# Keeping the products of |gate| and its sigmoid in the up stage of an attention and quantized-FFN kernel, gate signs parked apart, no sweeps on GpSimd

## The chip, the cores and the metric

One core of a Trainium2 chip. A core has TensorE (matmul), VectorE (DVE), ScalarE (ACT), GpSimd (POOL) and SyncE (SP, here the only engine that issues DMAs). The metric is the device time of one execution in microseconds.

## What is computed

x is 2 x 2048 x 512 in f32. A layer norm, cross attention against a context of 128 rows, a residual; then a layer norm, a gated feed-forward net whose weights are quantized in blocks of 32 and whose activations are rounded with one scale for the whole tensor, and a residual:

```
def act_qdq(x):
    qmax = 2.0 ** (ACT_BITS - 1) - 1.0
    scale = jnp.maximum(jnp.max(jnp.abs(x)) / qmax, 1e-12)
    return jnp.clip(jnp.round(x / scale), -qmax - 1.0, qmax) * scale
...
x = act_qdq(x)
up = act_qdq(x @ lpbq_dequant(w_up).T)
gate = act_qdq(x @ lpbq_dequant(w_gate).T)
sig = fixed_qdq_u16(jax.nn.sigmoid(gate))
gate = act_qdq(gate * sig)
o = act_qdq(gate * up)
return o @ lpbq_dequant(w_down).T
```

Each act_qdq needs the maximum of the absolute value over the whole tensor before one element can be rounded. gate, up, gate * sig and o are 4096 x 1536; each of them therefore needs a pass that finds a maximum and a later pass that uses it.

## The kernel before

A tensor of 4096 x 1536 is handled as NU = 48 tiles of 128 partitions x 1024 elements (512 KB in f32). Eight groups of 512 tokens (NG) have six tiles each (UPG). One tile of a product is one unit: 24 matmuls (two halves, four chunks of the contraction, three pairs of high and low f16 parts, L623).

The stages, in order of time:

- *Attention and norms* (to about 137 us), with the weights' quantization beside them.
- *Gate product* (gate, take_gate, gate_max, park_gate). TensorE computes unit after unit into two pairs of PSUM banks; ScalarE copies each out (L682), VectorE takes its maximum (L1100), SyncE stores it in gate_park in DRAM. Two groups also turn the up and down weights. At its end come the maximum over the partitions, an all-reduce on GpSimd (L404), and the scale ginv (quant_scale, L1070).
- *Up product*, in two passes over the gate beside it. Pass a, with up units 0 to 23, two gate tiles each: SyncE fetches a gate tile; GpSimd rounds it to int16 into Q (gate_int, L464); ScalarE takes the magnitude (sweep_a, L811) and the sigmoid (sigmoid, L816); VectorE rounds the sigmoid (L1137) and multiplies and takes the maximum in one instruction (act_max, L1149; the product is written and not used). Then the scale sinv. Pass b, with units 24 to 47: the sigmoid again (L825), its rounding, and the rounded gate * sig into Q, on VectorE for even tiles (L1156) and on GpSimd (L475, L478) and VectorE (L1162) for odd ones. Beside both, ScalarE copies each up unit out of PSUM (take_up), VectorE takes its maximum (up_max, L1132) and SyncE stores it in up_park (L290). Unit n may start in PSUM when unit n-2 is out. At the end: the scale uinv.
- *The maximum of o* (676 to 777 us), in which TensorE has nothing to do. SyncE reads the 48 up tiles back (L327) into a ring of six; ScalarE takes |up| (L865) and |Q| (L851) for three tiles of four and VectorE multiplies with the maximum (L1217); the fourth goes over GpSimd (L488) and VectorE (L1208, L1210). Then the scale oinv, and the down weights and first up tiles are loaded.
- *Down product*: SyncE reads each up tile again, ScalarE rounds it (up_int, L883), VectorE multiplies with Q (o_int, L1238), splits the result in two f16 parts (L1241, L1243), TensorE multiplies (L665), VectorE adds the residual (finish, L1249), SyncE stores.

SyncE's queue is one list in program order: a DMA behind a wait is not issued before that wait is over. The same holds on every engine. Q keeps gate * sig for all 48 tiles as int16 with its sign, in 24,576 words per partition; the up tiles don't fit beside it, so they are read back from DRAM twice.

## Time and profile before

| | us |
|---|---|
| three runs: median (lowest to highest) | 1036.32 (1035.14 to 1036.73) |
| the profiled execution, its own time | 1034.82 |
| its span | 1033.0 |
| gate product, about | 137 to 398 |
| up product, about | 398 to 676 |
| maximum of o, about | 676 to 777 |
| down product, about | 777 to 1033 |

The span is from the first to the last instruction that the profiler saw. The stages' ends are read from the first and last matmul of each. Times in the rows below count from the span's start.

### The profile page before, as it was taken

The numbers are of one execution on the slowest core, as the hardware profiler recorded it, in microseconds if no ns is written. First come the engines' busy times: TensorE is split into PE (matmuls) and PEld (weight loads), VectorE is DVE, ScalarE is ACT, GpSimd is POOL, SyncE is SP. The second block draws the span as 40 slices with busy tenths as digits, with TensorE's granted clock in tenths as the row PEclk, the third lists the DMA queues.
The fourth block names the chain that finished last, engine by engine and source line by source line (L and its number), as shares of the span: only waits on it lengthen the run. The fifth ranks groups of instructions, "written<-read, shape, count | busy, mean of one in ns | idle before, by whom it ended". The sixth has DMA issues, their size and how long they took to land.

```text
span 1033.0 us, 12734 instructions
## 1 busy us (share of the span) xinstructions
PE 885.3 (86%) x4344; PEld 443.5 (43%) x4344; DVE 691.8 (67%) x957; ACT 497.7 (48%) x621; POOL 307.8 (30%) x218
## 2 busy tenths in 40 slices
PE   7999779999999999889996999910008999999998
PEld 6788534445444544333342444400003444444443
DVE  4999967423352332999997999969989744456610
ACT  2489854123221323889995656558984311222100
POOL 0399800660048001546563556512110000000000
PEclk9999999999999999999999899965558999999999
DMA  9522342222522274678891234228999744456221
GB/s 349 241 113 94 123 163 102 102 102 95 210 103 102 82 264 164 227 245 260 279 274 78 102 134 191 102 84 308 302 336 329 233 149 141 154 203 203 81 81 41
DMA packets 47706, 179.32 MB, mean 174 GB/s; under 512 B 4784, under 2 KB 4784, under 8 KB 45488
## 3 DMA queue, kind: packets, MB, share of 16 engines
q1 hardware_dynamic: 47664, 178.80, 48.6%
q8 instruction: 21, 0.34, 0.1%
q14 instruction: 21, 0.17, 0.0%
HBM read 108.53 MB, written 70.25 MB: 173 GB/s over the span
## 4 chain that ended last, share of the span: by engine, by line
PE 69%; issue 13%; DVE 9%; ACT 4%; DMA 3%; POOL 1%; POOLq 0%; SPq 0%; ACTq 0%; DVEq 0%
PE ps L623 35%; PE ps L665 24%; PE ps L495 4%; DVE big L1217 3%; PE ps L556 2%; ACT big L816 2%; PE ps L573 2%; DVE big L1149 2%; ACT big L682 1%; DVE big L1208 1%; DMA big<-up_park 1%; DMA big<-gate_park 1%; PE ps L513 1%; DVE small L1137 1%; DMA big<-in_L_xattn_Wq_dram 1%
## 5 line engine op out<-in xcount | busy, mean ns | idle before, releaser
L623 PE MATMUL ps<-big 128*128 (+1 forms) x2304 | 507.4, 381 | 27.5 <-ACT big L682 22.7
L623 PEld LDWEIGHTS ps<-big 128*128 128x128 f16 x2304 | 223.8, 98 | 306.2 <-ACT big L682 30.0
L665 PE MATMUL ps<-big 128*128 128x512 f16 x1152 | 251.2, 382 | 101.7 <-DVE big L1243 101.7
L682 ACT ACTIVATE big<-ps 128x1024 f32<-128x1024 f32 (+2 forms) x216 | 163.8, 787 | 286.4 <-PE ps L623 208.8
L665 PEld LDWEIGHTS ps<-big 128*128 128x128 f16 x1152 | 113.0, 98 | 239.8 <-issue 105.4
L1100 DVE TENSOR_REDUCE small<-big 128x1 f32<-128x1024 f32 (+1 forms) x48 | 58.4, 1219 | 147.7 <-ACT big L682 147.6
L883 ACT ACTIVATE big<-big,small 128x1024 int16<-128x1024 f32 x48 | 55.0, 1148 | 152.2 <-DVE big L1238 145.6
L1249 DVE SCALAR_TENSOR_TENSOR big<-ps,small,big 128x1024 f32<-128x1024 f32 x16 | 20.5, 1284 | 118.9 <-PE ps L665 118.9
L464 POOL TENSOR_SCALAR big<-big,small 128x1024 int16<-128x1024 f32 x48 | 78.7, 1641 | 66.1 <-DMA big<-gate_park 57.2
L495 PE MATMUL ps<-small,big 128*128 128x128 f32 x456 | 64.2, 283 | 11.0 <-DMA big<-in_ctx_dram 4.6
L404 POOL PARTITION_ALL_REDUCE small<-small x9 | 3.3, 380 | 225.2 <-DVE small L930 118.8
L495 PEld LDWEIGHTS ps<-small,big 128*128 128x128 f32 x456 | 54.4, 145 | 24.6 <-ACT big L682 8.0
L1238 DVE SCALAR_TENSOR_TENSOR big<-big,small 128x1024 int16<-128x1024 int16 x48 | 61.4, 1278 | 1.2 <-ACT big L883 1.1
L1132 DVE TENSOR_REDUCE small<-big 128x1 f32<-128x1024 f32 (+1 forms) x48 | 57.9, 1206 | 0.0
L816 ACT ACTIVATE big<-big,small 128x1024 f32<-128x1024 int16 x48 | 54.9, 1143 | 5.3 <-POOL big L464 2.9
L1217 DVE CUSTOM_DVE_ANT_0 big<-big,small 128x1024 f32<-128x1024 int16 x36 | 53.7, 1535 | 0.5 <-ACT big L851 0.4
L825 ACT ACTIVATE big<-big,small 128x1024 f32 (+1 forms) x48 | 52.2, 1139 | 0.0
L1137 DVE TENSOR_SCALAR small<-big 128x1024 uint16<-128x1024 f32 x54 | 42.7, 791 | 11.4 <-ACT big L816 10.1
L865 ACT ACTIVATE big<-big,small 128x1024 int16<-128x1024 f32 x36 | 41.0, 1143 | 18.8 <-DMA big<-up_park 8.5
L811 ACT ACTIVATE small<-big,small 128x1024 int16<-128x1024 f32 x36 | 41.1, 1143 | 9.7 <-DVE small L1149 9.4
L475 POOL TENSOR_SCALAR big<-big,small 128x1024 f32<-128x1024 int16 x24 | 35.2, 1468 | 34.7 <-DVE big L1162 27.7
L1149 DVE CUSTOM_DVE_ANT_0 big<-small 128x1024 f32<-128x1024 int16 x24 | 39.9, 1663 | 0.9
(90 smaller groups left out, 850.4 us busy)
## 6 DMA issues: line engine op xcount, KB each, us to landing
big<-up_park SPq DMA_DIRECT2D x96, 512.0 KB, 4.7
gate_park<-big SPq DMA_DIRECT2D x48, 512.0 KB, 2.6
big<-gate_park SPq DMA_DIRECT2D x48, 512.0 KB, 4.2
up_park<-big SPq DMA_DIRECT2D x48, 512.0 KB, 2.7
big<-in_x_dram SPq DMA_DIRECT2D x8, 1024.0 KB, 17.6
x_park<-big SPq DMA_DIRECT2D x8, 1024.0 KB, 3.9
big<-x_park SPq DMA_DIRECT2D x16, 512.0 KB, 4.5
out_dram<-big SPq DMA_DIRECT2D x16, 512.0 KB, 2.7
```

Of the source, the lines that this page charges most:

```text
L464: nc.gpsimd.tensor_scalar(Q[:, v], gate_in(v % 6, v >= 36), col["ginv"], 1.0, ALU.mult, ALU.mult).then_inc(q_d, 1)
L495: return nc.tensor.transpose(dst, src, ident)
L623: mm = nc.tensor.matmul(ps[:, 2 * (n % 2) + j], w[:, a, k, o:o + P], XT[:, g, b, k], start=(k == 0 and a + b == 0), stop=(k == KC - 1 and ...
L665: mm = nc.tensor.matmul(ps[:, 4 * s + i], OT[:, s, a, c, i * P:(i + 1) * P], WD[:, b, c], start=(c == 0 and a + b == 0), stop=(c == OC - 1 ...
L682: return nc.scalar.activation(dst, src, ACT.Copy)
L816: nc.scalar.activation(gate_in(v % 6, v >= 36), Q[:, v], ACT.Sigmoid, scale=col["gsc"]).then_inc(sig_d, 1)
L883: nc.scalar.activation(qa[:, k % 2], ring6[:, s], ACT.Copy, scale=col["uinv"]).then_inc(uq_d, 1)
L1100: nc.vector.tensor_reduce(gcol[:, bass.ds(g * UPG + n, 1)], gate_out[:, n % 2], AX.X, ALU.max, apply_absolute_value=True).then_inc(g_mx, 1)
L1132: nc.vector.tensor_reduce(ucol[:, bass.ds(n, 1)], up_out[:, s], AX.X, ALU.max, apply_absolute_value=True).then_inc(u_mx, 1)
L1149: nc.vector.tensor_tensor_reduce(gate_in(v % 6, v >= 36), magnitude(v), sig_int(v), 1.0, scol[:, s:s + 1], ALU.mult, ALU.max, scol[:, s:s ...
L1217: nc.vector.tensor_tensor_reduce(ring5[:, k % 6], qa5[:, k % 4], qb5[:, k % 4], 1.0, ocol[:, c:c + 1], ALU.mult, ALU.max, ocol[:, c:c + 1] ...
L1238: nc.vector.scalar_tensor_tensor(qb[:, k % 2], qa[:, k % 2], col["oinv"], Q[:, n], ALU.mult, ALU.mult).then_inc(oq_d, 1)
```

## The change

- Each gate tile is swept once. The rounded gate (now on ScalarE for every third tile, on VectorE for the others), its magnitude (ScalarE), the sigmoid (ScalarE), the rounded sigmoid and the product with its maximum (VectorE) are made as before, but the product |gate| * sigmoid, in f32, is kept. When its scale is known it is only scaled and rounded (settle), on ScalarE and VectorE in turn.
- 23 products stay in SBUF on a "shelf" (the words of Q), 25 go to a "bench" (the words of the up product's input, as its groups are used up); the 16 of these that come first are stored in product_park and fetched back.
- The sweep takes three gate tiles per two up units, over up units 0 to 31; the scaling takes six tiles per unit, in units 33 to 40.
- The product has lost the gate's sign. So in the gate product ScalarE also makes the sign of each tile as int16 (ACT.Sign) and SyncE stores it in sign_park; the down product fetches it, and VectorE multiplies the rounded up tile with it before the product with Q.
- The last six gate tiles aren't fetched: ScalarE copies them to the shelf.
- The up product uses all eight PSUM banks, four units at a time, and doesn't wait for the gate product's evacuation, since units 0 and 1 go to the other banks.
- The last six up tiles stay on the bench. The maximum of o starts with them, and ten more are fetched ahead; |Q| needs no sweep since Q has no sign; VectorE's product goes to PSUM. The down weights come in six pieces between these loads.
- GpSimd keeps the all-reduces and has no sweep after the weights.

The core of the diff:

```
 KEPT = 23
 PARKED = 16
 A_UNITS = 32
 B_UNIT = 33
 STAY = 42
...
+        def steps(n):
+            return range((3 * n + 1) // 2, (3 * n + 4) // 2)
...
+            def park_product(i):
+                sp.wait_ge(a_mx, i + 1)
+                k = i - KEPT
+                need(sp, p_st[k % 4], 16 * (k // 4))
+                sp.dma_start(prod_d[k], place(i)).then_inc(p_st[k % 4], 16)
...
+            for n in range(A_UNITS):
+                if n:
+                    for i in steps(n - 1):
+                        if KEPT <= i < KEPT + PARKED:
+                            park_product(i)
+                if n in (8, 14):
+                    for i in range(KEPT + (n - 8) // 3, KEPT + (n - 8) // 3 + 2):
+                        bench_gate(i)
+                for i in steps(n + 1):
+                    if KEPT + 4 <= i < NU:
+                        bench_gate(i)
+                park_up(n)
...
-            for v in range(NU):
-                gate_int(v)
             all_max(6, "smx", "sall")
...
+            for n in range(2 * UPG):
+                if 2 <= n < 4:
+                    pe.wait_ge(g_ev, NU - 4 + n + 1)
+                need(pe, u_ev, n - 3)
+                raise_unit(n // UPG, n)
...
+                    nc.scalar.activation((sign_early if early else sign_late)[:, n % 2], dst, ACT.Sign).then_inc(sign_ev, 1)
...
+            def settle(q):
+                i = TURN[q]
+                if KEPT <= i < KEPT + PARKED:
+                    dve.wait_ge(p_ld[(i - KEPT) % 4], 16 * ((i - KEPT) // 4) + 16)
+                if q >= 2:
+                    d = TURN.index((q - 2) // 2)
+                    dve.wait_ge((bact_d, bdve_d)[d % 2], d // 2 + 1)
+                nc.vector.tensor_scalar(Q[:, half_of(q)], turned_from(i), col["sinv"], None, ALU.mult).then_inc(bdve_d, 1)
...
+            for n in range(NU):
+                if n < A_UNITS:
+                    for i in steps(n):
+                        if (i + 1) % 3 and i + 1 < NU:
+                            gate_int(i + 1)
+                        sig_int(i)
+                        gate_product(i)
...
+            for c in range(NU):
+                v = STAY + c if c < 6 else c - 6
+                b = 2 * (c % 4)
+                dve.wait_ge(ra_d, c + 1)
+                need(dve, o_mx, c - 1)
+                nc.vector.tensor_tensor_reduce(ps[:, b:b + 2].rearrange("p b w -> p (b w)"), r_abs[:, c % 4], Q[:, HALF[v]], 1.0,
+                                               ocol[:, c % 2:c % 2 + 1], ALU.mult, ALU.max,
+                                               ocol[:, c % 2:c % 2 + 1]).then_inc(o_mx, 1)
...
+                nc.vector.tensor_tensor(qa[:, k % 2], qa[:, k % 2], sign_in[:, k % 3], ALU.mult).then_inc(us_d, 1)
```

What stands in a row now, at three places. SyncE before, from the end of the gate product (L279 fetches gate tiles, L290 stores an up tile, a_mx counts products):

```order
L279 DMA big<-gate_park 128x1024 [waits g_mm]
L279 DMA big<-gate_park 128x1024
L290 DMA up_park<-big 128x1024 [waits u_ev,g_st1,g_st0]
L279 DMA big<-gate_park 128x1024 x2
L290 DMA up_park<-big 128x1024 [waits u_ev]
L279 DMA big<-gate_park 128x1024 [waits a_mx] x2
```

SyncE after, around up units 16 to 19 (L347 stores a product, L304 fetches a gate tile, L351 stores an up tile, p_st counts stored products):

```order
L351 DMA up_park<-big 128x1024 [waits u_ev]
L347 DMA product_park<-big 128x1024 [waits a_mx] x2
L304 DMA big<-gate_park 128x1024 [waits g_ld5,p_st0]
L304 DMA big<-gate_park 128x1024 [waits g_ld6,p_st1]
L351 DMA up_park<-big 128x1024 [waits u_ev]
L347 DMA product_park<-big 128x1024 [waits a_mx]
L304 DMA big<-gate_park 128x1024 [waits g_ld7,p_st2]
```

The product stores, with their waits for VectorE, now stand ahead of the gate loads, and one or two loads go with each up unit instead of two.

VectorE before, one up unit of the first pass (L1137 rounds a sigmoid, L1132 is up's maximum, L1149 product and maximum):

```order
L1137 TENSOR_SCALAR small<-big 128x1024 [waits a_mx,sig_d]
L1132 TENSOR_REDUCE small<-big 128x1 [waits u_ev]
L1137 TENSOR_SCALAR big<-big 128x1024 [waits a_mx,sig_d]
L1149 ISA big,small<-small 128x1024 [waits r_d,aq_d]
L1149 ISA small 128x1
```

VectorE after, an up unit with two gate tiles (L1220 rounds a gate tile, L1225 a sigmoid, L1231 product and maximum, L1213 up's maximum):

```order
L1220 TENSOR_SCALAR big<-big,small 128x1024 [waits sig_d,g_ld4]
L1225 TENSOR_SCALAR small<-big 128x1024 [waits a_mx,sig_d]
L1231 ISA big,small<-big,small 128x1024 [waits r_d,abs_d]
L1231 ISA small 128x1
L1220 TENSOR_SCALAR big<-big,small 128x1024 [waits sig_d,g_ld5]
```

The rounding of the next gate tile has come to VectorE, ahead of the current tile's sigmoid and product.

GpSimd before, at the end of the first pass (L464 rounds a gate tile, L404 is the all-reduce, L475 and L478 belong to the second pass):

```order
L464 TENSOR_SCALAR big<-big,small 128x1024 [waits a_mx,g_ld5]
L404 ISA
L404 ISA small<-small 128x1 [waits col_max]
L475 ISA
L475 TENSOR_SCALAR big<-big,small 128x1024 [waits u_mm,sinv_d]
```

GpSimd after, its end from the last step on the weights (L513) on (L499 is the all-reduce):

```order
L511 TENSOR_SCALAR big<-big 128x6144 [waits w_rnd]
L513 TENSOR_TENSOR big<-big,small 128x6144 [waits w_rnd]
L499 ISA
L499 ISA small<-small 128x1 [waits col_max] x4
L104 UNCONDITIONAL_BRANCH
```

The four last all-reduces stand in a row, with one instruction without operands (ISA) ahead of them all instead of one ahead of each and one behind each of three.

## Rows read from the trace of the kernel before

**Rows 1.** The page: busy times; two groups (busy, mean ns, idle before, releaser).
```profile
PE 885.3 (86%) x4344; PEld 443.5 (43%) x4344; DVE 691.8 (67%) x957; ACT 497.7 (48%) x621; POOL 307.8 (30%) x218
...
L623 PE MATMUL ps<-big 128*128 (+1 forms) x2304 | 507.4, 381 | 27.5 <-ACT big L682 22.7
...
L1249 DVE SCALAR_TENSOR_TENSOR big<-ps,small,big 128x1024 f32<-128x1024 f32 x16 | 20.5, 1284 | 118.9 <-PE ps L665 118.9
```
**Rows 2.** Busy time in stretches: length, each engine, TensorE clock, DMA share, GB/s.
```profile
137.00:398.00 261.00, 260.93 (x1248) 123.69 (x1248) 105.17 (x108) 73.89 (x81) 64.19 (x10) 0.99 0.34 134
398.00:676.00 278.00, 254.99 (x1152) 110.93 (x1152) 252.87 (x276) 202.68 (x194) 145.76 (x98) 0.98 0.56 189
676.00:777.00 101.00, 0.00 (x0) 0.00 (x0) 87.75 (x113) 78.02 (x76) 17.93 (x14) 0.52 0.77 268
777.00:1033.00 256.00, 251.21 (x1152) 113.02 (x1152) 129.61 (x158) 51.97 (x46) 0.00 (x0) 0.99 0.47 159
```
**Rows 3.** The chain that ended last, gate product: start, us, what.
```profile
366.85 31.09 PE ps L623 x144
```
**Rows 4.** Timeline, start of the up product: start, us, engine, what, idle before.
```profile
399.13 20.88 PE L623 MATMUL ps<-big 128*128 128x512 f16 x96 [1.21 <-ACT big L682]
...
400.61 0.38 POOL L404 PARTITION_ALL_REDUCE small<-small  x1 [69.28 <-DVE small L1124]
...
401.66 0.21 DVE L1070 TENSOR_SCALAR small<-small 128x1 f32<-128x1 f32 x1
...
409.72 7.98 POOL L464 TENSOR_SCALAR big<-big,small 128x1024 int16<-128x1024 f32 x6 [8.73 <-issue]
```
**Rows 5.** Timeline of one up unit in the first pass.
```profile
461.75 1.55 SPq L279 DMA_DIRECT2D big<-gate_park  x2
...
465.02 1.60 POOL L464 TENSOR_SCALAR big<-big,small 128x1024 int16<-128x1024 f32 x1 [0.59 <-DMA big<-gate_park]
465.55 2.14 DVE L1149 CUSTOM_DVE_ANT_0 big<-small 128x1024 f32<-128x1024 int16 x1
...
467.62 1.28 DVE L1149 CUSTOM_DVE_ANT_0 big<-big,small 128x1024 f32<-128x1024 int16 x1
467.73 1.55 SPq L279 DMA_DIRECT2D big<-gate_park  x2
467.79 1.15 ACT L811 ACTIVATE small<-big,small 128x1024 int16<-128x1024 f32 x1 [0.60 <-DVE small L1149]
...
468.83 0.68 DVE L1137 TENSOR_SCALAR small<-big 128x1024 uint16<-128x1024 f32 x1
468.85 1.00 ACT L682 ACTIVATE big<-ps 128x1024 f32<-128x1024 f32 x1
469.43 1.21 DVE L1132 TENSOR_REDUCE small<-big 128x1 f32<-128x1024 f32 x1
```
**Rows 6.** Timeline of TensorE, from its longest stop on.
```profile
569.88 105.82 PE L623 MATMUL ps<-big 128*128 x480 [8.43 <-ACT big L682]
```
**Rows 7.** Timeline, end of the up product: the scale's last step, GpSimd's first sweep.
```profile
681.86 0.21 DVE L1070 TENSOR_SCALAR small<-small 128x1 f32<-128x1 f32 x1
...
688.26 1.11 POOL L488 TENSOR_SCALAR big<-big,small 128x1024 int16<-128x1024 f32 x1 [7.07 <-issue]
```
**Rows 8.** Busy time in stretches, columns as in rows 2.
```profile
372.00:375.00 3.00, 3.00 (x16) 1.37 (x14) 1.22 (x1) 1.02 (x1) 0.00 (x0) 1.00 1.04 442
...
766.00:772.00 6.00, 0.00 (x0) 0.00 (x0) 5.22 (x9) 4.23 (x5) 0.00 (x0) 0.50 0.98 393
```
**Rows 9.** Timeline, from the last product to the first down matmul.
```profile
771.43 0.08 DVE L1217 DVE_READ_ACCUMULATOR2_ANT small<- 128x1 f32 x1
...
774.74 1.28 DVE L1238 SCALAR_TENSOR_TENSOR big<-big,small 128x1024 int16<-128x1024 int16 x1
...
776.52 0.69 DVE L1243 TENSOR_TENSOR big<-big 128x1024 f16<-128x1024 int16 x1
...
777.36 22.86 PE L665 MATMUL ps<-big 128*128 128x512 f16 x94 [101.66 <-DVE big L1243]
```

More of the change, by code:

```diff
@@ L271, in _ @@
                          wd_in.rearrange("(h p) n -> p h n", p=P)).then_inc(wn_ld[2], 16)
-            with nc.sync.Fori(4, NG - 1) as g:
+            for g in range(4, NG - 1):
                 park_gate(g)
@@ L363, in _ @@
                     fetch_x2(s + 1, r)
-            with nc.sync.Fori(1, 3) as t:
+            for t in range(1, 3):
                 for s in range(2):
@@ L373, in _ @@
                         fetch_x2(g + 1, r)
+            fetch_sign(NU - 1, (NU - 1) % 3)
             for g in range(NG - 2, NG):
@@ L869, in _ @@
-            for k in range(12):
-                if k % 4:
-                    magnitudes(0, k)
-            with nc.scalar.Fori(1, 4) as t:
-                for k in range(12):
-                    if k % 4:
-                        magnitudes(t, k)
+                act.wait_ge(u_st[s], 16 * STAY // 2)
+            for c in range(NU):
+                if c >= 6:
+                    act.wait_ge(c_ld[c % 8], 16 * ((c - 6) // 8) + 16)
+                need(act, o_mx, c - 3)
+                nc.scalar.activation(r_abs[:, c % 4], bench[:, HOLD[c % 16]], ACT.Abs, scale=col["uinv"]).then_inc(ra_d, 1)
@@ L1256, in _ @@
             finish(0, 0)
-            with nc.vector.Fori(1, 4) as t:
+            for t in range(1, 4):
                 for k in range(UPG):
```

507 lines of the change are left out of this document (261 added, 246 removed).

## The prediction

> **What bounds the kernel now.** I read the busy times of the page first: TensorE is busy 885 of 1033 us, so what it does not do is 148 us [rows 1]. Then the busy time by stage, to see where the rest lies: the gate product (137 to 398) is full, the down product (777 to 1033) is full, the up product (398 to 676) has about 23 us of idle TensorE, and from 676 to 777 TensorE does nothing at all while VectorE is busy 88 of 101 us [rows 2]. One unit of a product (24 matmuls) takes 5.18 us where nothing disturbs it (31.09 us for 144) [rows 3], so 48 units need 248.6 us. The up product took 276.6 us (399.1 to 675.7), 28.0 more. The page puts 22.7 us of it down to waiting for ScalarE's evacuation of PSUM [rows 1]. Three places pay for it.
>
> First, the two-engine sweep. With GpSimd beside it the product-and-maximum instruction takes 2.14 us, the next one, with GpSimd idle, 1.28 us [rows 5]; one up unit carries two gate tiles and the unit comes every 5.98 us instead of 5.18 (SyncE's pair of loads at 461.75 and 467.73) [rows 5]. Second, after each all-reduce GpSimd starts its next sweep late though its data are there: at 409.72 where the scale stood at 401.87 [rows 4], at 688.26 with 7.1 us of idle time that nothing in the profile explains [rows 7]. In the order excerpt on GpSimd an instruction without operands stands between the two, at the start of the second pass too, where TensorE has its longest stop, 8.43 us [rows 6]. Third, 676 to 777: every up tile is read back, and the maximum of |up| times |gate| is taken by VectorE.
>
> **The change, part by part.** Times are those of the profiled execution, 1034.8 us (span 1033.0).
>
> *Gate product: 0.* Each unit adds one Sign sweep on ScalarE (1.15 us at most, taken from its like 1.06 us apart in [rows 5]) and one half-size DMA. ScalarE is busy 74 of 261 us there [rows 2]; with 48 x 1.15 = 55 us more it is at 129, and TensorE works in the other two banks meanwhile. If the cover were gone, it would be 55 us.
>
> *Start of the up product: -1.2.* Units 0 and 1 go into the four banks that the gate product does not use, so the wait of 1.21 us [rows 4] goes.
>
> *Sweep per two up units, three gate tiles.* VectorE: three times rounding the sigmoid (0.60 start to start) and product (1.21), two gate roundings (0.60, bounded by 0.60 and 1.21, the same form of instruction as the first), two maxima (1.21): 9.05 us. ScalarE: three Abs, three Sigmoid, one rounding at 1.06, two PSUM copies at 1.00: 9.4 us [rows 5]. TensorE needs 10.36. So TensorE would be the bound, and ScalarE may be up to three units (15.5 us) late, since PSUM now holds four units instead of two; the copy itself takes 1.0, leaving 14.5 us. The slow start (scale at 401.87 [rows 4], then five sweeps and a table load) is about 6 us and within it.
>
> *What the new parking adds.* Between units 16 and 26 the queue of SyncE stores 16 products and must wait for each product before it issues the gate loads behind it. I follow one pair of units from ScalarE's first sweep at 0: second sigmoid done at 5.3, second product at 7.6 (VectorE: two roundings, a product, a gate rounding between). Behind it stand two product stores and the first load for the next pair. A load alone lands 3.3 us after issue (461.75 to 465.02 [rows 5]); each 512 KB ahead of it costs 1.33 us at the 393 GB/s of [rows 8] (0.524 MB / 393); with up's own store in the way, 0.3. So 7.6 + 2.7 + 3.3 + 0.3 = 13.9 us per pair, 3.5 more than TensorE's. Five such pairs: unit 26 is evacuated 1.0 + 69.5 + 6.3 = 76.8 us after the end of unit 15, and TensorE wants its banks at 14 x 5.18 = 72.5. **Stall 4.3 us**, and 1 us for the clock behind a stop (the stage's 28.0 less its 22.7 of waits is 5.3 for 22 stops, most behind the longest). Bounds: none if the pair takes 13.0 or less; 14.6 if it takes 15.9, which is eight tiles at the rate of before's sweep (three in 5.98 us).
>
> The Trainium skill, "DMA: Bandwidth & Descriptors", section "Where 436 GB/s comes from", says that about 358 GB/s of HBM bandwidth binds for one core; [rows 8] show 442 GB/s over 3 us and 393 over 6, so the measurement decides. By the skill's figure a tile takes 1.46 instead of 1.33 us: an estimate of 0.4 us more per pair, 2 in the stall, and 2 in the last stretch.
>
> *Second pass over the gate: 0.* It was four sweeps per tile on three engines (2.0 us of VectorE per tile and more); now it is one scaling of a kept product, on ScalarE or VectorE in turn: three each per up unit, 4.2 us with the copy, under 5.18. The wait for the scale (about 5 us) falls into the 14.5 us, and GpSimd's late start there with its stop of 8.43 us is gone. The 16 products come back in two bursts of 11 and 4; the last may be 3 us late, again covered.
>
> *End of the up product:* 397.94 + 248.6 + 4.3 + 1.0 = 651.9, against 675.7.
>
> *Stretch without TensorE.* Copy 1.0, maximum 1.2, reduction and hand-off 0.35, all-reduce to scale 1.26 (400.61 to 401.87 [rows 4]): 655.7; 3.8 after the last matmul; before it was 6.4 (675.70 [rows 6] to 682.07 [rows 7]). Abs 1.15: 656.9. Six up tiles never left SBUF and ten are loaded, so the 7.1 us of GpSimd and 1.2 of its sweep before the first product go. Then 48 products at 1.21: 715.0. They write PSUM, which no row of this form shows. Bounds: 1.28 start to start, as long as VectorE's instruction that reads PSUM lasts [rows 1], 3.4 us more; and 0.15 less than 1.21, since ScalarE's copy out of PSUM takes 1.00 where its sweeps in SBUF take 1.15 [rows 5], 7 us less. I take 1.21, the same instruction into SBUF. The loads: 32 tiles and six pieces of the down weights, 656.9 + 38 x 1.33 + 2.0 (3.3 less one transfer) + 2.5 for the last sweep and product: 712; at the stage's mean of 268 GB/s [rows 2] it would be 736. They run back to back as in [rows 8], so I take VectorE as the bound and 2 us for a load or two late: **717.0**. Before, this point was 771.5 [rows 9].
>
> *To the first down matmul.* Before 5.85 us (771.51 to 777.36) [rows 9]. Now the first up tile is loaded only when the last Abs is done (715.5 + 3.3 = 718.8), then rounding 1.15, the sign product 0.69 (as L1243 in [rows 9]), 0.2 of hand-offs and the 2.62 from the first product to the first matmul (774.74 to 777.36 [rows 9]): 723.4, 6.4 after the maximum.
>
> *Down product: 0.* VectorE gets 48 x 0.69 = 33 us more beside its 130 of 256; the loads of 48 sign tiles add 12.6 MB to 159 GB/s, 49 GB/s more [rows 2]. If the cover were gone: 33 us.
>
> **Sum.** 723.4 + 255.6 (777.36 to 1033.0) = 979.0 of span, +1.8 = 980.8 against 1034.8. The median of the runs before lies 1.5 above the profiled execution: **982 us**, 54 less.
>
> **Rivals.**
> 1. *No stall.* Loads land sooner than 13.0 us per pair allows, and the last stretch is at VectorE's bound: 982 - 5.3 - 2 = 975. For it: [rows 8] has 442 GB/s.
> 2. *The parking stretch runs at the old sweep's transfer rate,* 15.9 per pair: stall 14.6, 992. For it: stores and loads mixed ran at no more than that in the sweep of before [rows 5].
> 3. *VectorE stays slow without GpSimd.* If the 2.14 us comes from something else (DMA traffic, ScalarE), half of the products keep it: 0.43 more on average. The sweep becomes 10.3 per pair, still under TensorE; the last stretch gains 48 x 0.43 = 20.6: 1003. Against: 1.28 stands right behind 2.14, with the same DMA load [rows 5].
> 4. *Slower than before:* the two slots each of rounded gate, |gate| and rounded sigmoid make the engines take turns, one tile at a time: rounding 0.68, sigmoid 1.15, rounding 0.68, product 1.36, hand-offs 0.4 = 4.3 us per tile, 6.4 per unit, with copy and maximum 8.6; 32 units take 276 instead of 166 us, less 14.5 of slack: 1072. It decides from 7.5 us per unit on ((54 + 5.3 + 14.5) / 32 over 5.18). Against: the rounding for tile i+1 stands ahead of tile i's in VectorE's queue, as the order excerpt shows.
> 5. *The change does not do what it says:* ScalarE's and SyncE's new work cancels the gain, within 0.2% of 1036. It would need 54 us of stalls in stages that have cover.
>
> **How the numbers follow.** Forecast 0.55 (its own range 977 to 989), rival 1 0.17, rival 2 0.15, rival 3 0.08, rival 4 0.03, rival 5 0.01, and 0.01 for something else that is faster. Range 972 to 1001: it takes in rivals 1 and 2 and most of the last stretch's bounds. 0.2% (2 us) is about what a measurement can tell from no change. Faster 0.96, same 0.01, slower 0.03.
>
> **What would show it.** TensorE's stops in the up product: one group of them, after unit 27, 3 to 8 us together, and none where the second pass begins. The product instruction 1.28 us everywhere. GpSimd nearly empty, its last three all-reduces within 0.2 us of their maxima. From the last up matmul to the first down matmul about 71 us instead of 101.7. SyncE waiting for products between units 16 and 26. Wrong: TensorE stopping in every unit from the start (rival 4), product instructions over 1.4 us (rival 3), a gate product longer than 261 us, or VectorE idle on ScalarE idle on loads in the last stretch.

## The result, and the profile after

The changed kernel takes 987.31 us (median of four runs, 986.04 to 988.41) against 1036.53 (median of four, 1035.14 to 1039.24): a ratio of 0.952, with an interval of 0.950 to 0.955, 49 us less. The prediction was 982 with a range of 972 to 1001. The profiled execution took 986.25 us, 1.1 less than that median; its span is 984.5 us, against 1033.0 before.

The page of the changed kernel, its busy times and the two groups of VectorE that hold the product with the maximum (busy, mean ns of one, idle before and its releaser), beside TensorE's group of the up product:

```profile
PE 884.0 (90%) x4344; PEld 446.4 (45%) x4344; DVE 634.0 (64%) x989; ACT 517.1 (53%) x637; POOL 145.5 (15%) x110
...
L720 PE MATMUL ps<-big 128*128 (+1 forms) x1152 | 253.9, 383 | 9.6 <-ACT big L760 9.6
...
L1231 DVE CUSTOM_DVE_ANT_0 big<-big,small 128x1024 f32<-128x1024 int16 x48 | 61.6, 1284 | 7.3 <-ACT big L912 0.5
...
L1274 DVE CUSTOM_DVE_ANT_0 ps<-big,small 128x1024 f32<-128x1024 int16 x48 | 58.0, 1285 | 1.2 <-ACT big L955 1.2
```

TensorE is busy as before [rows 1], now 90% of a shorter span. GpSimd lost 162 of 308 us. Every product lasts 1.28 us, in the up stage and in the last stretch, where it writes PSUM.

The busy time of the changed kernel by stage (length, each engine, TensorE clock, DMA share, GB/s), to be laid beside [rows 2]:

```profile
137.00:397.00 260.00, 260.00 (x1248) 123.59 (x1247) 104.33 (x105) 120.58 (x125) 64.16 (x10) 0.99 0.48 185
397.00:660.00 263.00, 253.43 (x1152) 113.28 (x1151) 187.44 (x260) 194.97 (x186) 0.73 (x2) 0.98 0.66 241
660.00:729.00 69.00, 0.60 (x4) 0.14 (x2) 64.86 (x114) 58.10 (x52) 0.70 (x2) 0.54 0.96 363
729.00:984.00 255.00, 251.01 (x1152) 113.14 (x1150) 161.68 (x204) 51.69 (x45) 0.00 (x0) 0.99 0.56 201
```

TensorE's own timeline in the changed kernel, from the up product on (start, us, what, idle before):

```profile
396.99 134.84 PE L720 MATMUL ps<-big 128*128 128x512 f16 x624
532.54 10.53 PE L720 MATMUL ps<-big 128*128 x48 [0.70 <-ACT big L760]
547.63 13.05 PE L720 MATMUL ps<-big 128*128 x48 [4.56 <-ACT big L760]
562.90 12.22 PE L720 MATMUL ps<-big 128*128 x48 [2.22 <-ACT big L760]
575.42 10.53 PE L720 MATMUL ps<-big 128*128 x48 [0.30 <-ACT big L760]
587.74 72.69 PE L720 MATMUL ps<-big 128*128 x336 [1.79 <-ACT big L760]
```

The up product runs 26 units without a stop, then stops five times (9.6 us), and after 587.74 it takes 72.7 us for 14 units, the undisturbed 5.19 each. The third and fourth rows show the other loss: 48 matmuls that elsewhere take 10.5 us took 13.05 behind the stop of 4.56 us, and the next 48 took 12.22 behind one of 2.22 us.

So the 48.5 us of span came from these places, each the difference of two timelines:

| | before | after | change |
|---|---|---|---|
| start of the up product | 399.13 | 396.99 | -2.1 |
| up product | 276.6 | 263.4 | -13.1 |
| no TensorE work: up to the first product | 13.8 | 5.2 | -8.6 |
| the 48 products with maximum | 82.0 | 58.0 | -24.0 |
| last product to first down matmul | 5.85 | 5.2 | -0.6 |
| down product | 255.6 | 255.7 | 0.0 |

The 2.1 us at the start of the up product are only partly the change. The gate product takes the same time in both (260.9 us without the wait of 1.21 that is gone), and it begins at 136.07 instead of 136.96, behind the attention stage; in the experiments below, none of which has an edit ahead of that point, it begins between 136.1 and 138.8. So 0.9 of the 2.1 is within the scatter.

Two thirds of the gain lie in the stretch in which TensorE waits for everything else. The 24.0 us of the products come out of VectorE's rows. Before, 36 tiles took a product of 1.535 us in the mean, some of them beside GpSimd, where it is 1.285 now (9.0 us), and twelve tiles took two instructions (L1208 and L1210, 1.22 us each) where one of 1.21 us is enough now (14.8 us).

More than half of what was possible in the up product was not had: 263.4 stands against the 248.6 of 48 undisturbed units and the 276.6 of before, and that is what most experiments are about.

How those 14.8 us come about is told by ScalarE, which sweeps three gate tiles for every two up units. Its first sweep of a pair (L907) starts at 441.27, 450.96, 460.66, 470.63 and 480.99, some 10 us apart, and from then on at the times below, where it waits for a gate tile to land. Timeline of ScalarE in the changed kernel:

```profile
496.00 1.15 ACT L907 ACTIVATE big<-big,small 128x1024 int16<-128x1024 f32 x1 [4.55 <-DMA big<-gate_park]
510.96 1.15 ACT L907 ACTIVATE big<-big,small 128x1024 int16<-128x1024 f32 x1 [5.15 <-DMA big<-gate_park]
525.86 1.15 ACT L907 ACTIVATE big<-big,small 128x1024 int16<-128x1024 f32 x1 [5.09 <-DMA big<-gate_park]
540.96 1.15 ACT L907 ACTIVATE big<-big,small 128x1024 int16<-128x1024 f32 x1 [5.29 <-DMA big<-gate_park]
556.13 1.15 ACT L907 ACTIVATE big<-big,small 128x1024 int16<-128x1024 f32 x1 [5.37 <-DMA big<-gate_park]
568.75 1.15 ACT L907 ACTIVATE big<-big,small 128x1024 int16<-128x1024 f32 x1 [2.82 <-DMA big<-gate_park]
581.07 1.15 ACT L907 ACTIVATE big<-big,small 128x1024 int16<-128x1024 f32 x1 [2.51 <-DMA big<-gate_park]
...
586.68 1.00 ACT L760 ACTIVATE big<-ps 128x1024 f32<-128x1024 f32 x1
```

Five pairs take 75.1 us (480.99 to 556.13), 15.0 each, in the stretch where products are stored; the next two take 12.6 and 12.3, with no product left to store. The copy that starts at 586.68 frees the banks of unit 30, and TensorE starts unit 34 at 587.74. Undisturbed it would have started it at 396.99 + 34 x 5.18 = 573.1. The whole loss is 14.6 us at this point, and it is set by when ScalarE comes to the copies, thus by the gate loads.

What SyncE waited for in the up product of the changed kernel (line, releaser: us in total, times, longest):

```profile
SPq L351 <- ACT big L760: 178.4, 37, 9.4
...
SPq L347 <- DVE small L1231: 6.2, 8, 1.1
```

SyncE is held above all by the store of an up unit, L351, which waits for ScalarE's copy; the gate loads stand behind it. The waits for products (L347), which the prediction put in the middle of the matter, sum to 6.2 us. Most of the 178.4 lies in units where SyncE is merely early; in the five slow pairs (481 to 556) it is 43.1 us.

### The profile page after: what moved, and what is told of

Its sections match the earlier page's. It is cut to its first block, busy times and chain, and to the rows that moved or that the text cites. A ratio compares the mean times of both kernels' runs of the same rounds, so it can differ in the third digit from the quotient of the medians.

```text
span 984.5 us, 12109 instructions
## 1 busy us (share of the span) xinstructions
PE 884.0 (90%) x4344; PEld 446.4 (45%) x4344; DVE 634.0 (64%) x989; ACT 517.1 (53%) x637; POOL 145.5 (15%) x110
## 4 chain that ended last, share of the span: by engine, by line
PE 73%; issue 10%; DMA 7%; DVE 5%; ACT 4%; SPq 1%; POOLq 0%; POOL 0%; DVEq 0%; ACTq 0%
PE ps L744 26%; PE ps L686 25%; PE ps L720 15%; DMA big<-gate_park 4%; PE ps L558 4%; PE ps L619 2%; DMA big<-in_L_ffn_w_gate_dram 2%; PE ps L636 2%; ACT big L912 1%; ACT big L760 1%; DVE small L1225 1%; SPq L270 1%; DMA product_park<-big 1%; DVE big L1061 1%; ACT big L920 1%
## 5 line engine op out<-in xcount | busy, mean ns | idle before, releaser
L744 PE MATMUL ps<-big 128*128 128x512 f16 x1152 | 251.2, 381 | 68.4 <-DVE big L1300 68.4
L720 PE MATMUL ps<-big 128*128 (+1 forms) x1152 | 253.9, 383 | 9.6 <-ACT big L760 9.6
L686 PE MATMUL ps<-big 128*128 128x512 f16 (+1 forms) x1152 | 252.6, 381 | 4.7 <-DVE big L1164 4.7
L1181 DVE TENSOR_REDUCE small<-big 128x1 f32<-128x1024 f32 (+1 forms) x48 | 58.4, 1219 | 148.1 <-ACT big L760 148.0
L963 ACT ACTIVATE big<-big,small 128x1024 int16<-128x1024 f32 x48 | 55.0, 1148 | 156.4 <-DVE big L1295 131.7
L499 POOL PARTITION_ALL_REDUCE small<-small x9 | 3.3, 363 | 522.9 <-DVE small L1253 194.7
L1213 DVE TENSOR_REDUCE small<-big 128x1 f32<-128x1024 f32 x48 | 58.1, 1215 | 28.9 <-ACT big L760 28.9
L558 PE MATMUL ps<-small,big 128*128 128x128 f32 x456 | 64.4, 283 | 10.5 <-DMA big<-in_ctx_dram 4.6
L1231 DVE CUSTOM_DVE_ANT_0 big<-big,small 128x1024 f32<-128x1024 int16 x48 | 61.6, 1284 | 7.3 <-ACT big L912 0.5
L1274 DVE CUSTOM_DVE_ANT_0 ps<-big,small 128x1024 f32<-128x1024 int16 x48 | 58.0, 1285 | 1.2 <-ACT big L955 1.2
L955 ACT ACTIVATE big<-big,small 128x1024 int16<-128x1024 f32 x48 | 53.7, 1144 | 4.9 <-DVE small L1150 2.9
L912 ACT ACTIVATE big<-big,small 128x1024 int16<-128x1024 f32 x48 | 54.5, 1135 | 0.0
L877 ACT ACTIVATE big<-big 128x1024 int16<-128x1024 f32 x48 | 50.8, 1059 | 2.1 <-DMA sign_park<-big 1.2
L1225 DVE TENSOR_SCALAR small<-big 128x1024 uint16<-128x1024 f32 x48 | 32.9, 686 | 12.9 <-ACT big L920 12.8
```

The source lines that it names most:

```text
L558: return nc.tensor.transpose(dst, src, ident)
L686: mm = nc.tensor.matmul(ps[:, 2 * (n % 2) + j], w[:, a, k, o:o + P], XT[:, g, b, k], start=(k == 0 and a + b == 0), stop=(k == KC - 1 and ...
L720: mm = nc.tensor.matmul(ps[:, b + j], WU[:, a, k, o:o + P], XT[:, g, c, k], start=(k == 0 and a + c == 0), stop=(k == KC - 1 and c == 1))
L744: mm = nc.tensor.matmul(ps[:, 4 * s + i], OT[:, s, a, c, i * P:(i + 1) * P], WD[:, b, c], start=(c == 0 and a + b == 0), stop=(c == OC - 1 ...
L912: nc.scalar.activation(g_abs[:, i % 2], place(i), ACT.Abs, scale=col["ginv"]).then_inc(abs_d, 1)
L1181: nc.vector.tensor_reduce(gcol[:, bass.ds(g * UPG + n, 1)], shelf[:, SHELF[n]] if kept else gate_out[:, n % 2], AX.X, ALU.max, apply_absol ...
```

## The experiments

The theory after the result, A: the up product is late only because each gate load is asked for too late, by its place in SyncE's queue. Its rival, B: the DMA engines have no room for loads and stores together, and an earlier request changes nothing. Beside that, two losses of the kernel before are tested by putting them back (GpSimd beside VectorE, GpSimd changing its work), and the change to eight banks by itself.

### Gate loads ahead of the product stores

```
             for n in range(A_UNITS):
+                if n >= 18:
+                    for i in steps(n + 1):
+                        if i < NU:
+                            bench_gate(i)
                 if n:
...
-                for i in steps(n + 1):
-                    if KEPT + 4 <= i < NU:
-                        bench_gate(i)
+                if n < 18:
+                    for i in steps(n + 1):
+                        if KEPT + 4 <= i < NU:
+                            bench_gate(i)
```

> The changed kernel, but from up unit 18 on SyncE issues the gate loads of the next unit ahead of the stores of the products (same tiles, same bytes). Theory A, the stops come from the chain product, store issue, load: in the changed kernel ScalarE's first sweep of a pair comes every 14.96, 14.90 and 15.10 us (496.00, 510.96, 525.86, 540.96), the loads are issued 8.7 us into the pair and land 6.2 us later, behind two stores. With the loads at about 6.6 us into it and only an up store ahead they land near 11.5, so the pair comes at 11.5 or at TensorE's 10.4; TensorE's stops in the up product go from 9.6 us to 0 to 2, the half clock behind them (5.2 us) goes too, and the time is 13 to 15 us less, 972 to 975. Theory B, the transfers themselves are the bound (8 tiles a pair, as many bytes as before): the pair stays at 14 to 15 us and the time within 2 us of the changed kernel's 987.3.

Measured: 977.76 us (976.22 to 980.21), 0.944 of the kernel before (0.940 to 0.947), 9.5 less than the changed kernel. From unit 18 on the loads are asked for before the product stores; nothing else differs. TensorE in this kernel:

```profile
397.34 155.56 PE L725 MATMUL ps<-big 128*128 128x512 f16 x720
553.70 10.53 PE L725 MATMUL ps<-big 128*128 x48 [0.80 <-ACT big L765]
566.10 10.53 PE L725 MATMUL ps<-big 128*128 x48 [1.87 <-ACT big L765]
578.50 72.69 PE L725 MATMUL ps<-big 128*128 x336 [1.86 <-ACT big L765]
```

The stops fell from 9.6 to 4.5 us, and behind them every 48 matmuls take 10.53 us: no slowed ones. The direction is A's, but the time missed A's 972 to 975, because the pairs didn't come down to TensorE's pace. Timeline of one pair in this kernel (SPq is SyncE's DMA issue):

```profile
496.35 1.15 ACT L912 ACTIVATE big<-big,small 128x1024 int16<-128x1024 f32 x1 [4.55 <-DMA big<-gate_park]
...
503.00 0.34 SPq L351 DMA_DIRECT2D up_park<-big  x1
503.44 1.21 SPq L304 DMA_DIRECT2D big<-gate_park  x2
504.74 0.93 SPq L347 DMA_DIRECT2D product_park<-big  x2
...
508.88 1.15 ACT L912 ACTIVATE big<-big,small 128x1024 int16<-128x1024 f32 x1 [2.73 <-DMA big<-gate_park]
```

The loads still stand behind the previous up unit's store (L351), which is issued 6.7 us after the pair began, when ScalarE's copy is done; the first of them lands 5.4 us after its issue. 7.1 + 5.4 = 12.5 us per pair. The last two pairs of the changed kernel, with no product to store, have the same shape and the same length: loads issued at 563.19, tile landed at 568.75, 12.6 us. What remained was thus the distance of one unit between request and use, not the products.

### Gate loads two units ahead

```
+            ahead = {17: 28, 18: 29, 19: 32}
+            asked = KEPT + 3
             for n in range(A_UNITS):
+                until = ahead.get(n, min(NU - 1, steps(n + 2)[-1])) if n >= 17 else asked
+                if n > 17:
+                    for i in range(asked + 1, until + 1):
+                        bench_gate(i)
...
-                for i in steps(n + 1):
-                    if KEPT + 4 <= i < NU:
+                if n == 17:
+                    for i in range(asked + 1, until + 1):
                         bench_gate(i)
+                asked = until
```

> The changed kernel with the gate loads of the sweep ahead of the product stores and issued two up units ahead instead of one (from unit 19 on, as slots come free; same tiles, same bytes). With the loads only moved ahead of the stores the pair went from 15.0 to 12.5, 13.1 and 12.5 us, not to 10.4 to 11.5 as expected: the loads landed 5.4 us after issue. Theory A, still waiting for single loads, slowed by the stores issued right behind them: with two units of lead every load has 10 us to land, the pair comes at TensorE's 10.4 to 10.8, the stops shrink to under 1.5 us, and the time is 970 to 973. Theory B, the bytes bound it (8 tiles per pair at what stores and loads mixed can do): the pair stays at 12 us or more and the time within 2 us of the 977.8 of the loads-first version.

Measured: 974.36 us (971.87 to 975.08), 0.939 (0.935 to 0.944), 13 less than the changed kernel. The up product of this kernel is one row of TensorE's timeline; the second row is the stretch that was the worst (columns as in the table by stage), the third what the DMA queue moved in slices of 1.75 us from 490 to 560 us:

```profile
399.63 248.80 PE L727 MATMUL ps<-big 128*128 128x512 f16 x1152
```

```profile
500.00:560.00 60.00, 60.00 (x280) 27.20 (x279) 47.31 (x66) 48.88 (x46) 0.00 (x0) 1.00 0.91 326
```

```profile
GB/s 154 400 339 297 162 337 368 318 30 283 302 274 300 417 424 339 126 316 391 138 215 382 421 403 126 302 419 147 225 391 410 351 304 417 419 421 417 424 419 419
```

248.80 us for 48 units is the undisturbed pace. The DMA queue moves 326 GB/s here; the changed kernel moved 289 (490 to 560). Since the same bytes go through in less time when they are asked for earlier, the DMA engines had room in the changed kernel, and B falls as the cause of its 15.0 us per pair. A isn't borne out in full either. ScalarE's first sweeps of a pair come at 498.65, 510.67, 520.37, 534.64, 547.28 and 557.88, 11.8 us apart in the mean and not TensorE's 10.4 to 10.8. ScalarE still waits for loads, up to 2.2 us at a time, SyncE now waits 28.8 us for product stores to land, and from about 548 on the queue moves 417 to 424 GB/s without a gap. What sets these 11.8 us, the last slots or by then the bytes, isn't shown. TensorE doesn't feel it: five such pairs are about 7 us late together, and the four units in PSUM give 14.5 us. The time, 974.36, lies between what A (970 to 973) and B expected.

The up product gave back all 14.6 us. The median fell by less, 13, and the span by 11.5, because in this execution the up product began at 399.63 and not 396.99. That lies ahead of every edit: the gate product already began at 138.83 and not at 136.07. (The kernel before, run beside this one, was 1.5 us lower too, 1035.0.)

### PSUM for two units instead of four

```
-                need(pe, u_ev, n - 3)
+                need(pe, u_ev, n - 1)
...
-                    pe.wait_ge(u_ev, 2 * UPG * t + n - 3)
+                    pe.wait_ge(u_ev, 2 * UPG * t + n - 1)
```

> The changed kernel with one part undone: TensorE waits until unit n-2 is out of PSUM, as before, instead of n-4; banks, sweeps and loads stay as changed. By the account of the prediction, the slack goes from 14.5 to 4.1 us, so the five pairs of the parking stretch (4.6 us late each) stop TensorE for 20 us instead of 9.6, and the slow start of the sweep (first evacuation at 409.1 where it was ready at 402.2) for 2 to 3 us: 10.4 + 2.5 and about 2 of half clock more, 1002. If the evacuations were late only because TensorE had run ahead, it would be the 987 of the changed kernel.

Measured: 1000.43 us (996.92 to 1002.91), 0.965 (0.960 to 0.971), 13 more than the changed kernel. This is the changed kernel with the depth of before: a unit may start when the one two ahead of it is out. TensorE in this kernel, the first stops:

```profile
409.19 93.40 PE L720 MATMUL ps<-big 128*128 128x512 f16 x432 [1.73 <-ACT big L760]
504.52 10.53 PE L720 MATMUL ps<-big 128*128 x48 [1.93 <-ACT big L760]
519.65 13.17 PE L720 MATMUL ps<-big 128*128 x48 [4.60 <-ACT big L760]
```

The first stop comes after the first two units, the next at 504.5, 28 us earlier than in the changed kernel. 1002 was expected by the account of the prediction, and 987 if the depth had made no difference. The stops sum to 20.3 us instead of 9.6. These 10.7 us are about the two units of depth (10.4 us of TensorE's work), and most of the 13. So the depth is worth what the sweep is late, up to those units.

The up product of this kernel ends at 673.0 and takes 276.1 us, as long as in the kernel before (276.6). So the single sweep alone, with its loads in this order, gained nothing in this stage; it took the depth beside it.

### The kernel before with four units in PSUM

```
+            for n in range(2 * UPG):
+                if 2 <= n < 4:
+                    pe.wait_ge(g_ev, NU - 4 + n + 1)
+                need(pe, u_ev, n - 3)
+                raise_unit(n // UPG, n)
...
-                copy(up_out[:, s], ps[:, 2 * s:2 * s + 2].rearrange("p b w -> p (b w)"))
+                copy(up_out[:, s], ps[:, b:b + 2].rearrange("p b w -> p (b w)"))
```

> The kernel before with one part of the change: the up product has four units in PSUM instead of two, and its first two don't wait for the gate product's evacuation. The sweeps stay as they were. If TensorE's stops before (22.7 us) are a lateness of the sweep that adds up at 0.8 us a unit, two more units of slack (10.4 us) and the 1.2 us of the start are all that this part gives: 1036.5 - 11.6 = 1025. If the lateness is mostly GpSimd's two late starts (which more slack swallows once each), the gain is up to 22: 1015. If ScalarE's and VectorE's pace of 5.98 us a unit simply moves the stops, it is 1.2: 1035.

Measured: 1032.24 us (1030.4 to 1035.14, ten runs), 0.996 (0.994 to 0.998): 4 us less than the 1036.5 of the kernel before. That is nearest to the third of the cases expected, 1035, in which the stops only move. TensorE and VectorE in this kernel:

```profile
570.83 96.16 PE L657 MATMUL ps<-big 128*128 x432 [8.41 <-ACT big L698]
...
775.92 14.42 PE L681 MATMUL ps<-big 128*128 128x512 f16 x54 [108.93 <-DVE big L1265]
```

```profile
677.59 1.21 DVE L1154 TENSOR_REDUCE small<-big 128x1 f32<-128x1024 f32 x1
```

TensorE ends its up product at 570.83 + 96.16 = 667.0, 8.7 us earlier than before (675.7 [rows 6]), and then stands idle 108.9 us instead of 101.7. VectorE's last sweep ends at 678.8, no sooner than before (678.2). The last step of the scale behind it starts at 680.22, where it was 681.86 before [rows 7], only because the all-reduce was no longer late: GpSimd had ended its last sweep at 671.4, where in the kernel before it ended at 674.9 and the all-reduce came 5.95 us behind it, 2.4 us after its data. These 1.6 us are all that the two timelines show (the profiled executions differ by 1.3 us, the medians by 4). So in the kernel before TensorE's stops were a symptom: the sweeps' own work set the end of the stage, and room in PSUM alone only moved the waiting. With the sweeps of the change the same room is worth 13 us (the experiment above).

### GpSimd sweeps put back beside the last products

```
             all_max(7, "umx", "uall")
+            idle = part(43008, 1024)
+            pool.wait_ge(uinv_d, 1)
+            nc.gpsimd.memset(idle, 0.0).then_inc(idle_d, 1)
+            for c in range(NU - 4):
+                need(pool, o_mx, c)
+                need(pool, idle_d, c + 1)
+                nc.gpsimd.tensor_scalar(idle, idle, 1.0, 1.0, ALU.mult, ALU.mult).then_inc(idle_d, 1)
...
+                if c == NU - 1:
+                    dve.wait_ge(idle_d, NU - 3)
                 nc.vector.tensor_tensor_reduce(
```

> The changed kernel with 44 sweeps on GpSimd (128x1024 f32, multiplied by 1, on words that nobody uses) beside VectorE's products in the maximum of o; they are waited for only by the last product. Theory A, VectorE's product is held up by GpSimd: each product under a sweep takes 2.07 us start to start instead of 1.21, so about 44 x 0.86 = 38 us more, 1025. Theory B, the 2.1 us before came from the transfers or from ScalarE: the products stay at 1.21 and the time at 987, though the transfers are as dense as in any stretch (379 GB/s).

Measured: 1024.58 us (one run), 37 more than the changed kernel. It adds 44 sweeps on GpSimd, whose results aren't used, in the stretch in which VectorE is the bound. Timeline of this kernel at the place where they begin (the second kind of row is VectorE's product, the DVE_READ rows left out):

```profile
672.36 1.29 DVE L1284 CUSTOM_DVE_ANT_0 ps<-big,small 128x1024 f32<-128x1024 int16 x1
673.00 1.55 POOL L559 TENSOR_SCALAR big<-big 128x1024 f32<-128x1024 f32 x1 [8.20 <-issue]
...
673.57 2.06 DVE L1284 CUSTOM_DVE_ANT_0 ps<-big,small 128x1024 f32<-128x1024 int16 x1
674.71 1.81 POOL L559 TENSOR_SCALAR big<-big 128x1024 f32<-128x1024 f32 x1 [0.15 <-POOL big L559]
...
675.55 2.05 DVE L1284 CUSTOM_DVE_ANT_0 ps<-big,small 128x1024 f32<-128x1024 int16 x1
...
757.25 1.29 DVE L1284 CUSTOM_DVE_ANT_0 ps<-big,small 128x1024 f32<-128x1024 int16 x1 [4.60 <-POOL big L559]
...
762.85 0.38 POOL L500 PARTITION_ALL_REDUCE small<-small  x1 [5.77 <-issue]
```

The product lasts 1.29 us until GpSimd starts and 2.05 from then on; both engines settle at one of each per 1.97 us, though the product writes PSUM and reads other words than the sweep. TensorE's idle stretch grew from 68.4 to 107.8 us, 39.4. It divides into three: the product's extra 0.77 us some 40 times (30.8), 4.6 us in which the last product waits for the last sweep (a wait that the edit put in), and 4.0 us by which the all-reduce comes later behind the last product (4.4 us from 758.46 to 762.85 instead of 0.4). Theory A's 38 us was thus met partly by luck: 31 of the 39 are the held-up products, and the other two terms weren't in it. The Trainium skill, "SBUF — State Buffer", section "SBUF: two separate sides", says that an instruction of VectorE with two inputs in SBUF and one of GpSimd that reads SBUF shut each other out for their whole length. This trace agrees nearly: a product started at 675.55 beside the sweep of 674.71 to 676.52 and ended at 677.60, 1.08 us after that sweep, where a product alone lasts 1.28.

### GpSimd given one other instruction between two all-reduces

```
             all_max(7, "umx", "uall")
+            pool.wait_ge(col_all, 8)
+            nc.gpsimd.tensor_scalar(col["uall"], col["uall"], 1.0, 1.0, ALU.mult, ALU.mult).then_inc(same_d, 1)
...
-            dve.wait_ge(col_all, 8)
+            dve.wait_ge(same_d, 1)
```

> The changed kernel with one multiplication of one column on GpSimd between the all-reduce of the up maximum and the scale; VectorE's scale waits for it. Its work is under 0.3 us. Theory A, GpSimd pays about 7 us for going from the all-reduce to an ordinary instruction (7.6 and 7.1 us of unexplained idle time before): 7 to 8 us more, 994 to 995, and nothing more at the next all-reduce, 60 us later. Theory B, the late starts came from the loads and waits of the old sweeps: 0.3 us more, 987.6.

Measured: 995.89 us (995.41 to 997.99), 0.961 (0.957 to 0.965), 8.6 more than the changed kernel: theory A, with a delay somewhat longer than the 7 to 8 us expected. The edit adds a multiplication of one column by one behind the all-reduce whose scale starts the last stretch. GpSimd in this kernel:

```profile
664.69 0.35 POOL L500 PARTITION_ALL_REDUCE small<-small  x1 [67.77 <-DVE small L1266]
673.96 0.19 POOL L554 TENSOR_SCALAR small<-small 128x1 f32<-128x1 f32 x1 [8.93 <-issue]
```

The multiplication itself lasts 0.19 us and starts 8.93 us after the all-reduce, with its data there. The delay doesn't depend on the size of the instruction: it was 8.73 and 7.07 us before full tiles in the kernel before [rows 4, 7], 8.20 in the experiment above. In the same experiment a memset directly behind the all-reduce started without such a delay (at 663.85, with 0.94 us of waiting for the scale), and the way back, from sweeps to an all-reduce, cost 5.77. The next all-reduce of this kernel, 60 us later, came 0.47 us after the last product, as without the edit (0.42): the way back was over by then.

Between these two rows the view of line L554 has one more (count, shortest, median and longest in ns, first and last start):

```profile
L554 POOLq MODIFY_POOL_CONFIG  x2: 83/83/83, 665.0 to 665.0; - x2
```

Such a pair of instructions, MODIFY_POOL_CONFIG, stands on GpSimd's queue at each of these late starts: at 400.9, 554.8 and 681.1 in the kernel before ahead of its sweeps, at 675.1 and 762.9 ahead of its all-reduces, at 664.8 and 757.3 in the experiment above. There is none ahead of the memset, and none after 330.9 in the changed kernel. They last 0.08 us or less each, so the time passes behind them. The prediction called the 7.1 us idle time that nothing in the profile explains; this pair is what the profile shows there.

### TensorE kept at work before the down product

```
-                b = 2 * (c % 4)
+                b = 2 * (c % 2)
...
+            idle = part(HT0, 512).bitcast(F16)
+            pe.wait_ge(o_mx, 36)
+            for m in range(70):
+                nc.tensor.matmul(ps[:, 4 + m % 4], idle[:, 0:P], idle[:, 0:512], start=True, stop=True)
             pe.wait_ge(o_mx, NU)
```

> The version with loads two units ahead, and TensorE does 70 idle matmuls (128x128 by 128x512, results not used) between product 36 of the maximum of o and the first down matmul; VectorE's products use four PSUM banks instead of eight for that. In the changed kernel 41 recorded matmuls at the start of the down product took 11.38 us, 0.28 us each, at a granted clock of 0.5 rising to 1.0, where 0.216 is the full-clock step. Theory A, that half clock costs what these rows say (11.38 - 41 x 0.216 = 2.5 us, missing records aside) and work ahead of it avoids it: 2 to 3 us less than the version without. Theory B, VectorE's first units (3.1 us each) are what TensorE follows there, so a faster clock gains under 0.5 us.

Measured: 972.85 us (971.28 to 973.54), 0.938 (0.934 to 0.943). It is the kernel with loads two units ahead, with 70 matmuls added whose results aren't used, and the products in four banks instead of eight:

```profile
697.25 17.06 PE L759 MATMUL ps<-big 128*128 128x512 f16 x70 [48.84 <-DVE small L1285]
716.82 63.36 PE L751 MATMUL ps<-big 128*128 128x512 f16 x285 [2.50 <-DVE big L1311]
```

The down stage took 255.0 us instead of 256.2. From its first matmul to 722.0 the granted clock was 0.67 with 17 matmuls recorded, where it was 0.50 with 13 in the kernel without them; by 728 the lead was 5 matmuls, 1.1 us at 0.216 each. So the added work, which ended 2.5 us ahead of the stage, shortened the time at the lower clock and didn't avoid it. The medians differ by 1.5 us in the same direction, but their runs overlap (971.9 to 975.1 and 971.3 to 973.5), so this lies between the two expectations and is a hint, not a finding. It is the fastest version run, 63 us below the kernel before; nearly all of what it has over the changed kernel is the order of SyncE's loads.

## Why the prediction was right, and where its terms were off

The time came out 5.3 us above the forecast, inside the forecast's own range (977 to 989), and the gains lie where they were put. The sizes are less sure than the total makes them look: two errors partly cancelled (below). Step by step:

1. **Gate product: nothing.** Right. The stage took 260.9 us with ScalarE busy 121 of them, where 129 was the estimate.
2. **Start of the up product.** -1.2 was predicted and came; a further 0.9 lies ahead of the gate product and is scatter between executions.
3. **The stall: 4.3 us and 1.0 for the clock were predicted, 14.8 us measured.** This is the step that failed. Two terms were off. The pair of units with parking was put at 13.9 us and took 15.0, which over five pairs is 5.6 us (75.1 against 69.5): the second product was done 8.3 us into the pair instead of 7.6 (510.96 to 519.2), because rounding and sigmoid wait for one another and for their tile, and the next tile landed 6.6 later instead of 6.3. And the sum stopped at the last product that is parked. The loads still stood behind the store of the up unit there, so that the next two pairs took 24.9 us instead of TensorE's 20.7, another 4.2. Together 9.8, against 9.5 missed. The stops began at unit 26 and came to 9.6 us, where the sign named was one group after unit 27 of 3 to 8 us. The prediction's picture of what gates a load was thus too narrow: it named the product, and the experiment with the loads ahead of the products removed only half of the stops. The 3.3 us from issue to landing was also the better of two: in [rows 5] it is the first load of a pair, and the second, with the up store behind it, landed 5.2 us after its issue.
4. **The clock.** Predicted as 1.0 us on top of the stops. Behind the stop of 4.56 us TensorE's granted clock was 0.50, the lower of its two levels, from 547.6 to 552: seven matmuls from 547.63 on took 3.17 us, 0.45 each, where they take 0.22. It came to 5.2 us in all (253.9 of the page against 248.7). But these aren't added to the loss: TensorE restarts at 587.74 when the copy of unit 30 is done, whatever it did in between, and after that only 0.2 us is missing. The slow matmuls took the place of stops. So the 1.0 added for the clock was a term with no loss of its own behind it.
5. **Second pass: nothing.** Right. No stop after 587.74; GpSimd's late start and the 8.4 us stop of [rows 6] are gone.
6. **Last stretch: 71.5 predicted, 68.4 measured.** First product 5.2 after the last matmul, where 5.0 was said. The products came at 1.205 us start to start, the value taken, though they write PSUM: 58.0. The 2 us set aside for late loads weren't needed: VectorE never waited. After the last product 5.2 us instead of 6.4, because ScalarE's |up| ran three tiles ahead and ended 3.5 us before the maximum, so that the first up tile was asked for at 720.20 and had landed; I had it end 1.5 ahead.
7. **Down product: nothing.** Right: 255.7 with 32 us more of VectorE's work and 42 GB/s more traffic.

The last stretch begins and ends in these rows of the changed kernel's timeline:

```profile
665.64 1.29 DVE L1274 CUSTOM_DVE_ANT_0 ps<-big,small 128x1024 f32<-128x1024 int16 x1 [1.20 <-ACT big L955]
...
723.56 0.14 DVE L1274 DVE_READ_ACCUMULATOR2_ANT small<- 128x1 f32 x1
...
728.84 1.44 PE L744 MATMUL ps<-big 128*128 128x512 f16 x3 [68.40 <-DVE big L1300]
```

The two errors, 9.5 us too little in the up product and 3.1 too much behind it, partly cancelled, which is luck; with -0.9 for the start they make the 5.5 us between the predicted span of 979.0 and 984.5.

**The rivals.** Rival 2 (15.9 per pair, 992 us) came nearer than the forecast did, in its pair (15.0 was measured; the forecast had 13.9) and by a little in its time (987.3 is 4.7 us from it and 5.3 from the forecast). Its reason, a queue that moves no more than in the sweep of before, fell with the loads issued two units ahead: there eight tiles went by in 11.8 us. Rival 1 (no stall, 975) is what that experiment gave (974.4), though its reason too, loads that land sooner, isn't what did it: they landed hardly sooner (6.2 us in the median of the slow stretch, against 6.8 in the changed kernel) and were asked for earlier. Rival 3 (VectorE slow without GpSimd) fell: 1.28 us everywhere, and 2.05 as soon as GpSimd sweeps again. Rival 4 (engines taking turns) fell: pairs in the undisturbed part took 9.7 us, under TensorE's 10.4. I was wrong on one more point, in the first part: I counted TensorE's 22.7 us of stops in the kernel before as what the up stage cost; the run with four units in PSUM shows that taking a third of them away was worth 4 us at most, since the sweeps ended no sooner.

The rule by which HBM would bind at 358 GB/s (the Trainium skill, "DMA: Bandwidth & Descriptors", section "Where 436 GB/s comes from") isn't borne out for this core, which ran alone: the last stretch of the changed kernel moved 363 GB/s over its whole 69 us, and its slices from 490 on in the up product reached 426. The traffic there was uneven, as these slices of 1.75 us show (DMA busy in tenths, GB/s; the changed kernel, 490 to 560 us):

```profile
DMA  9998970399999960799879922999999606999899
GB/s 403 281 255 328 417 321 35 129 396 356 255 215 372 426 258 5 309 400 297 190 260 419 421 101 103 398 368 253 208 389 417 267 5 255 400 302 250 246 419 419
```

Once in every pair the queue runs dry (35, 5, 101, 5 GB/s), 15 us apart: the sign of requests that come late, not of a full queue. In a prediction this pattern would be read off the order of SyncE's queue.

## What to carry to other kernels

Count for each load what its queue holds ahead of it, stores that wait for another engine included, and give it the distance in units that covers its landing time and that wait; here moving requests, with the same bytes, was worth 12 to 13 us. A stop of the busiest engine names its releaser, not the bound: deeper buffering gave 4 us where the sweeps were the bound and 13 where they were only late. Taking the last sweeps off GpSimd pays twice, once in VectorE's products (1.21 us start to start instead of 1.97 beside a sweep) and once for each change between its all-reduce and its sweeps.

## What the runs showed of the hardware that I had not expected

- GpSimd's change from an all-reduce to a multiplication cost 7.0 to 8.9 us, for one column as for a full tile; the way back 5.8 and 5.95, and 10.5 at the end of the kernel before (762.70 to 773.20, of which 1.5 us lay behind the maximum); a memset behind the all-reduce had no such delay. A pair of MODIFY_POOL_CONFIG stands at each.
- VectorE's two-input product goes from one per 1.21 us to one per 1.97 us beside a sweep of GpSimd, even when its output is in PSUM.
- A gate tile that shares the queue with an up store just ahead of it and a second load just behind it lands 5.4 to 5.6 us after its issue, where the row of before, a first load with its store 2.2 us behind it, had 3.3 [rows 5]. Product stores behind it or none made no difference. Which of the neighbours costs the 2 us wasn't measured apart.
- After a stop of 4.56 us TensorE ran its next matmuls at 0.45 us each instead of 0.22, and after the next one, of 2.22 us, again (12.22 us for 48, granted clock 0.52 in the first 3.1 us); after stops of 1.9 us and less it didn't (10.53 us for 48).
